# The last tile's mean taken from the matrix product, through two more weight columns

## The reference

```
logits = einsum('bsh,he->bse', hidden_states, gate_w)
routing_weights, _ = top_k(logits, 2)
h = relu(einsum('bsh,hi->bsi', hidden_states, up_w)) ** 2
shared_out = einsum('bsi,ih->bsh', h, down_w)
x_latent = einsum('bsh,hl->bsl', hidden_states, fc1_w)
expert_out = einsum('bsl,lm->bsm', x_latent, expert_w)
moe_out = expert_out * sum(routing_weights, axis=-1, keepdims=True)
routed_out = einsum('bsl,lh->bsh', moe_out, fc2_w)
return _layernorm(shared_out + routed_out, ln_gamma, ln_beta)   # over 512 values
...
x + _L0_ffn_ref(_L0_cond_ref(x, ...), ...)
```

## Time and profile before

| | us |
|---|---|
| median of three runs | 256.61 |
| span of the profiled execution, first to last instruction | 254.6 |
| median of the runs less that span | 2.0 |
| PE busy | 248.0 |
| DVE busy | 155.8 |
| ACT busy | 81.8 |
| POOL busy | 39.4 |

### The profile page before, as it was taken

How to read it: one execution, slowest core, us unless ns; L and a number is a source line. 1 busy time by engine, 2 the same in 40 slices (tenths; PEclk the granted TensorE clock), 3 DMA queues, 4 the chain that set the end, 5 groups by cost and what they waited for, 6 DMA issues and landing times.

```text
span 254.6 us, 3526 instructions
## 1 busy us (share of the span) xinstructions
PE 248.0 (97%) x1291; PEld 207.1 (81%) x1291; DVE 155.8 (61%) x272; ACT 81.8 (32%) x142; POOL 39.4 (15%) x45
## 2 busy tenths in 40 slices
PE   8999999999999999999999999999999999999992
PEld 7877887988888888888888888888888888788891
DVE  4798999944448964644447983464444953406453
ACT  4669856411003452321112534331111355202100
POOL 2400021000117120001114411001111700001110
PEclk9999999999999999999999999999999999999997
DMA  6994804001111400001111220000011100000111
GB/s 161 332 324 153 305 17 153 0 0 44 41 41 41 167 0 0 3 0 42 41 41 41 78 87 0 0 0 11 31 41 44 42 0 0 0 3 8 74 44 41
DMA packets 10444, 15.60 MB, mean 61 GB/s; under 512 B 1088, under 2 KB 4928, under 8 KB 10432
## 3 DMA queue, kind: packets, MB, share of 16 engines
q1 hardware_dynamic: 9984, 15.33, 17.6%
q10 hardware_dynamic: 448, 0.11, 0.2%
HBM read 11.23 MB, written 4.20 MB: 61 GB/s over the span
## 4 chain that ended last, share of the span: by engine, by line
PE 89%; DMA 3%; issue 2%; DVE 1%; SPq 1%; ACT 0%; POOL 0%; POOLq 0%; DVEq 0%
PE ps L932 27%; PE ps L934 27%; PE ps L933 27%; PE ps L906 4%; DMA late<-in_up_w_dram 3%; PE ps L998 2%; PE ps L950 1%; PE ps L956 1%; PE ps L952 1%; SPq L322 0%; POOL rstd L417 0%; DVE stats L714 0%; DVE y_buf L712 0%; DVE h_full L636 0%; ACT h_hi L474 0%
## 5 line engine op out<-in xcount | busy, mean ns | idle before, releaser
L932 PE MATMUL ps<-down_hi,sq_hi 128*128 128x512 f32 (+1 forms) x136 | 51.2, 377 | 0.0
L933 PE MATMUL ps<-down_lo,sq_hi 128*128 128x512 f32 (+1 forms) x136 | 51.2, 377 | 0.0
L934 PE MATMUL ps<-down_hi,sq_lo 128*128 128x512 f32 (+1 forms) x136 | 51.2, 376 | 0.0
L932 PE MATMUL ps<-h_hi,up_hi 128*128 128x512 f32 x120 | 46.8, 390 | 0.0
L934 PE MATMUL ps<-h_hi,up_lo 128*128 128x512 f32 x120 | 46.7, 389 | 0.0
L933 PE MATMUL ps<-h_lo,up_hi 128*128 128x512 f32 x120 | 46.7, 389 | 0.0
L417 POOL TENSOR_TENSOR rstd<-mv,half 128x1 f32<-128x1 f32 x16 | 15.3, 954 | 158.2 <-DVE mv L719 153.2
L512 ACT ACTIVATE relu_sq<-ps 128x512 f32<-128x512 f32 x32 | 19.1, 597 | 57.7 <-PE ps L934 44.3
L712 DVE TENSOR_TENSOR y_buf<-ps,y_buf 128x512 f32<-128x512 f32 x15 | 10.4, 692 | 41.0 <-PE ps L934 40.7
L685 DVE CAST sq_hi<-relu_sq 128x512 fp32r<-128x512 f32 x32 | 22.6, 706 | 16.2 <-ACT relu_sq L514 15.7
L932 PEld LDWEIGHTS ps<-down_hi,sq_hi 128*128 128x128 f32 x136 | 25.6, 188 | 4.7
(11 more groups left out here) (137 smaller groups left out, 308.7 us busy)
## 6 DMA issues: line engine op xcount, KB each, us to landing
out_dram<-late SPq DMA_DIRECT2D x15, 256.0 KB, 2.0
x_cur<-in_x_dram SPq DMA_DIRECT2D x3, 1024.0 KB, 5.2
late<-in_down_w_dram SPq DMA_DIRECT2D x4, 512.0 KB, 5.3
late<-in_up_w_dram SPq DMA_DIRECT2D x3, 512.0 KB, 8.8
x_cur<-in_x_dram SPq DMA_DIRECT2D x2, 512.0 KB, 7.2
experts_sb<-in_experts_dram SPq DMA_DIRECT2D x3, 256.0 KB, 3.5
agg_b<-aggb_dram SPq DMA_DIRECT2D x1, 768.0 KB, 4.9
latents_sb<-in_latents_dram SPq DMA_DIRECT2D x1, 528.0 KB, 4.8
```

What stands on the lines that cost most here:

```text
L932: nc.tensor.matmul(dst, a_hi, b_hi, start=first, stop=False)
L933: nc.tensor.matmul(dst, a_hi, b_lo, start=False, stop=False)
L934: return nc.tensor.matmul(dst, a_lo, b_hi, start=False, stop=last)
```

## The change

The mean of a token over its 512 outputs is the product of its activations with the row sums of the weights, over 512. The change keeps each row sum, split into high and low part and written twice, as columns 512 and 513 of `down_hi`, `down_lo`, `q_hi` and `q_lo`. These rows become 514 values long (2056 bytes in place of 2048). The sums are made by DVE in block 0, between its four `normalise` calls.

In the last tile the half with columns 256 to 511 now comes first, and its 30 products are 258 wide: the two columns more hold the sum over all 512 outputs. The gamma step of this half then needs nothing of the other half. The gamma step of the other half stands right behind the joint statistics and does not wait for them; only `rstd` still does. The order of the two stores is exchanged too.

```diff
+            def sum_rows(weights, at, n, part):
+                nc.vector.tensor_reduce(row_sums[:, part, at:at + n], weights[:, :, 0:HID].bitcast(fp32), AX.X,
+                                        ALU.add).then_inc([hi_summed, lo_summed][part], 1)
+
+            def split_sums():
...
+                nc.vector.tensor_copy(down_hi[:, :, HID:HID + 2], row_sums[:, 0, 0:IC].unsqueeze(2).to_broadcast([P, IC, 2])
+                                      ).then_inc(sum_hi_ready, 1)
...
+                def times_gamma(i):
+                    cols = halves[i]
+                    nc.vector.scalar_tensor_tensor(out=y[:, cols], in0=last_shared(i), scalar=last_mean[:, :],
+                                                   in1=gamma_b[:, cols], op0=ALU.subtract,
+                                                   op1=ALU.mult).then_inc(gamma_done, 1)
...
+                        nc.vector.tensor_scalar(last_mean[:, :], LAST_MEAN, 1.0 / HID, None,
+                                                ALU.mult).then_inc(last_mean_ready, 1)
+                        dve.wait_ge(last_mean_ready, 1)
+                        times_gamma(0)
                 dve.wait_ge(eps_added, 1)
                 dve.wait_ge(stats_done, n + 1)
                 nc.vector.bn_aggr(out=mv[:, :], in_=last_stats[:, :, :]).then_inc(mv_done, 2)
-                dve.wait_ge(mv_done, 2 * n)
-                for i, cols in enumerate(halves):
-                    nc.vector.scalar_tensor_tensor(out=y[:, cols], in0=last_shared(i), scalar=mv[:, 0:1],
-                                                   in1=gamma_b[:, cols], op0=ALU.subtract,
-                                                   op1=ALU.mult).then_inc(gamma_done, 1)
+                times_gamma(1)
...
-            for t in range(TB):
-                normalise(0, t)
+            normalise(0, 0)
+            sum_rows(down_hi, 0, IC, 0)
+            normalise(0, 1)
+            sum_rows(down_lo, 0, IC, 1)
+            normalise(0, 2)
+            sum_rows(q_hi, IC, LC, 0)
+            sum_rows(q_lo, IC, LC, 1)
+            split_sums()
+            normalise(0, 3)
...
                     if last_block and t == TB - 1:
                         pe.wait_ge(last_lo_ready, LC)
+                        pe.wait_ge(sums_ready, 3)
                         for half in (0, 1):
-                            cols = slice(half * HID // 2, (half + 1) * HID // 2)
+                            cols = LAST_COLS[half]
+                            dst = [shared(TB - 1)[:, 0:HID // 2 + 2], last_shared(1)][half]
```

More of the change, by code:

```diff
@@ L88, in adaln_ffn_kernel @@
         up_lo = sb("up_lo", [P, HC, INT], f32r)
-        down_hi = sb("down_hi", [P, IC, HID], f32r)
-        down_lo = sb("down_lo", [P, IC, HID], f32r)
+        down_hi = sb("down_hi", [P, IC, HID + 2], f32r)
+        down_lo = sb("down_lo", [P, IC, HID + 2], f32r)
         fc1_hi = sb("fc1_hi", [P, HC, LAT], f32r)
         fc1_lo = sb("fc1_lo", [P, HC, LAT], f32r)
-        q_hi = sb("q_hi", [P, LC, HID], f32r)
-        q_lo = sb("q_lo", [P, LC, HID], f32r)
+        q_hi = sb("q_hi", [P, LC, HID + 2], f32r)
+        q_lo = sb("q_lo", [P, LC, HID + 2], f32r)
         h_hi = sb("h_hi", [P, HC, TOK], f32r)
@@ L117, in adaln_ffn_kernel @@
         mv = sb("mv", [P, 2])
+        row_sums = sb("row_sums", [P, 2, IC + LC])
+        last_mean = sb("last_mean", [P, 1])
         rstd = sb("rstd", [P, 1])
@@ L202, in routed @@
             return ps[:, 6 + t % 2, :]
+        LAST_COLS = [slice(HID // 2, HID + 2), slice(0, HID // 2)]
         def last_shared(half):
             return [shared(TB - 1), ps[:, LAT_BANK[0], :]][half][:, 0:HID // 2]
+        LAST_MEAN = shared(TB - 1)[:, HID // 2:HID // 2 + 1]
         mlp_loaded = [sem(f"mlp_loaded{i}") for i in range(2)]
@@ L305, in adaln_ffn_kernel @@
         gamma_done = sem("gamma_done")
+        hi_summed = sem("hi_summed")
+        lo_summed = sem("lo_summed")
+        rows_summed = sem("rows_summed")
+        sum_hi_ready = sem("sum_hi_ready")
+        sums_ready = sem("sums_ready")
+        last_mean_ready = sem("last_mean_ready")
         final_done = sem("final_done")
@@ L357, in _ @@
             for half in (0, 1):
-                cols = slice(half * HID // 2, (half + 1) * HID // 2)
+                cols = [slice(HID // 2, HID), slice(0, HID // 2)][half]
                 sp.wait_ge(final_done, NT + half)
@@ L533, in down_high @@
                 act.wait_ge(down_loaded[i], 16)
-                nc.scalar.copy(down_hi[:, ks, :], down_raw[:, ks, :]).then_inc(down_hi_ready, 1)
+                nc.scalar.copy(down_hi[:, ks, 0:HID], down_raw[:, ks, :]).then_inc(down_hi_ready, 1)
             for m in range(IC):
@@ L729, in normalise @@
                                                op1=ALU.add).then_inc(final_done, 1)
+            def sum_rows(weights, at, n, part):
+                nc.vector.tensor_reduce(row_sums[:, part, at:at + n], weights[:, :, 0:HID].bitcast(fp32), AX.X,
+                                        ALU.add).then_inc([hi_summed, lo_summed][part], 1)
+            def split_sums():
+                dve.wait_ge(hi_summed, 2)
+                dve.wait_ge(lo_summed, 2)
+                nc.vector.tensor_tensor(row_sums[:, 0, :], row_sums[:, 0, :], row_sums[:, 1, :], ALU.add
+                                        ).then_inc(rows_summed, 1)
+                dve.wait_ge(rows_summed, 1)
+                nc.vector.tensor_copy(down_hi[:, :, HID:HID + 2], row_sums[:, 0, 0:IC].unsqueeze(2).to_broadcast([P, IC, 2])
+                                      ).then_inc(sum_hi_ready, 1)
+                nc.vector.tensor_copy(q_hi[:, :, HID:HID + 2], row_sums[:, 0, IC:IC + LC].unsqueeze(2).to_broadcast([P, LC, 2])
+                                      ).then_inc(sum_hi_ready, 1)
+                dve.wait_ge(sum_hi_ready, 2)
+                nc.vector.tensor_tensor(down_lo[:, :, HID:HID + 2], row_sums[:, 0, 0:IC].unsqueeze(2).to_broadcast([P, IC, 2]),
+                                        down_hi[:, :, HID:HID + 2].bitcast(fp32), ALU.subtract).then_inc(sums_ready, 1)
+                nc.vector.tensor_tensor(q_lo[:, :, HID:HID + 2], row_sums[:, 0, IC:IC + LC].unsqueeze(2).to_broadcast([P, LC, 2]),
+                                        q_hi[:, :, HID:HID + 2].bitcast(fp32), ALU.subtract).then_inc(sums_ready, 2)
             def normalise_last():
@@ L735, in normalise_last @@
                 y = y_buf[:, t % 2, :]
-                halves = [slice(0, HID // 2), slice(HID // 2, HID)]
+                halves = [slice(HID // 2, HID), slice(0, HID // 2)]
+                def times_gamma(i):
[3 more added lines that the diff above has]
+                                                   op1=ALU.mult).then_inc(gamma_done, 1)
                 for i, cols in enumerate(halves):
@@ L763, in down_low @@
                 dve.wait_ge(down_hi_ready, i + 1)
-                nc.vector.tensor_tensor(down_lo[:, ks, :], down_raw[:, ks, :], down_hi[:, ks, :].bitcast(fp32),
+                nc.vector.tensor_tensor(down_lo[:, ks, 0:HID], down_raw[:, ks, :], down_hi[:, ks, 0:HID].bitcast(fp32),
                                         ALU.subtract).then_inc(down_lo_ready, 1)
@@ L1012, in down_product @@
                         pe.wait_ge(last_lo_ready, LC)
+                        pe.wait_ge(sums_ready, 3)
                         for half in (0, 1):
-                            cols = slice(half * HID // 2, (half + 1) * HID // 2)
+                            cols = LAST_COLS[half]
+                            dst = [shared(TB - 1)[:, 0:HID // 2 + 2], last_shared(1)][half]
                             for lc in range(LC):
-                                three_products(last_shared(half), lat_hi[:, lc, rows], lat_lo[:, lc, rows],
+                                three_products(dst, lat_hi[:, lc, rows], lat_lo[:, lc, rows],
                                                q_hi[:, lc, cols], q_lo[:, lc, cols], lc == 0, False)
                             for m in range(IC):
-                                last = three_products(last_shared(half), sq_hi[:, m, rows], sq_lo[:, m, rows],
+                                last = three_products(dst, sq_hi[:, m, rows], sq_lo[:, m, rows],
                                                       down_hi[:, m, cols], down_lo[:, m, cols],
@@ L1036, in down_product @@
                         last = three_products(shared(t), sq_hi[:, m, rows], sq_lo[:, m, rows],
-                                              down_hi[:, m, :], down_lo[:, m, :], m == 0, m == IC - 1)
+                                              down_hi[:, m, 0:HID], down_lo[:, m, 0:HID], m == 0, m == IC - 1)
                     last.then_inc(shared_done, 1)
```

6 lines of the change are left out of this document (3 added, 3 removed).

## The result

The changed kernel takes 261.04 us (median of 5 runs, 260.62 to 261.26) against 256.63 for the kernel before in the same session (256.14 to 256.71). The ratio is 1.0175, 95% interval 1.0162 to 1.0187. The forecast was 256.4 us, in a range from 255.9 to 257.2: wrong, and on the side of the rival "the shifted rows", which had 0.09. The granted clock of PE is 0.997 in the profiled execution, before 0.995, so the clock does not explain the loss.

The account below looks back on a forecast made before the run. PE, busy 248.0 of 254.6 us, was taken to bound the kernel, leaving its start, products and tail. The tail's -0.22 and wider products' +0.025 gave -0.20, from 256.61 to 256.4 us; range 255.9 to 257.2.

Parts of the forecast that it names:

- the shifted rows: Rival, chance 0.09: products starting off a 16 byte multiple take longer; at the upper bound +3.3 - 0.20, 259.7 us.
- The tail: Behind PE's last product: final steps start 0.22 us earlier, 1.54 us after it, released by POOL's power at 0.55.
- Wider products: Last tile on PE: two columns more in 30 products cost 0.025 us, bounds nothing and 3.2 us.
- DVE in block 0: Sums of 4.38 us delay tile 3's start to near 77.6; PE's slack covers it, price nothing.
- Longer rows: PE's products with q and down read rows 2056 bytes apart, 255 of them odd rows; taken as costing nothing.
- The bound: Upper limit for Longer rows: the fixed part of a product once more, 255 x 0.0128 = 3.3 us.
- The sign of being wrong: Forecast wrong if down stage products stand further apart than up stage ones, PE waits in block 1, or last power takes 0.98.
- The line rule: SBUF lines of 16 bytes: an odd row touches one line more, estimated 0.11 us, making the sum -0.09.
- a part of 0.04: Chance left for what the prediction did not see, with all buffers behind `down_hi` moving by up to 192 bytes.

Follow-up runs that it names:

- e9_rows256: Changed kernel with `down` and `q` rows of 576 values, eight start-up buffers moved into `early`, all operand distances 0 modulo 256 bytes; 256.35 us, ratio 0.9988.
- e1_h_place: Kernel before with one unused buffer of 64 bytes a partition ahead of `h_hi`, moving it and all behind it; 260.49 us, ratio 1.0148.
- e3_rows64: Changed kernel with `down` and `q` rows of 528 values in place of 514, so every row starts on a multiple of 64 bytes; 258.72 us, ratio 1.0087.
- e5_gap128: Kernel before with an unused gap of 128 bytes ahead of `h_hi`, so up, latent and down products are at distance 128; 261.50 us, ratio 1.0205.
- e4_all_place: Kernel before with a 64 byte buffer ahead of the first buffer, so all move together and keep their distances; 256.49 us, ratio 0.9998.
- e2_h_back: Changed kernel with a 64 byte buffer ahead of `h_hi`, putting it and all behind it back on a multiple of 128; 259.20 us, ratio 1.0099.
- e6_gap192: Kernel before with an unused gap of 192 bytes ahead of `h_hi`: up and latent products at distance 192, down at 64; 260.01 us, ratio 1.0137.

## Why the prediction was wrong

- **The tail** was right: 1.53 us against 1.54, the power the last to come, at 0.55, and one gamma step hidden behind PE's second half.
- **Wider products** were right in size: 258 columns cost nothing visible. In `e9_rows256`, where every distance is 0, the half with 258 columns takes 3.59 us, as the one with 256 did before.
- **DVE in block 0** was right: the sum 4.41 us against 4.38; tile 3 at 78.53 against 77.6, and 0.9 of that is PE's lag, with which tile 0 came already (its final step at 58.68 in place of 57.78); no wait of PE.
- **Longer rows** is the step that failed. It put this term of the sum at nothing, where PE's products took some 4.5 us more. It took nothing on the ground that all products shown keep the same distance in time whatever they read. That ground was empty: in the kernel before every pair of operands lies at a distance of 0 modulo 256, so its trace had one case only, and could not tell that the case matters. The step also counted the wrong products. It looked at the odd rows (255) and at the start against a multiple of 16 bytes; the runs show that rows on multiples of 64 lose as much, that one common shift loses nothing, and that all 930 products of 512 columns were at stake, more than half of them (480 up and latent ones) reading nothing that was changed.
- **The bound** of 3.3 us rested on that count, and on an assumed price, the fixed 12.8 ns of a product once more. No mean price in the table is that high; it is the count that took the loss past the bound. With the measured prices it is 384 x 6.5 ns (up) + 96 x 2.1 (latent) + 360 x 4.6 (down) + 90 x 3.9 (q) = 4.7 us. From the chain and the products behind it there are 0.76 + 3.71 + 0.34 = 4.81, or 4.5 without the 0.28 of start-up.
- **The rival of shifted rows**, with 0.09, had the direction and not the mechanism. It has a product slow when its operand starts off a multiple of 16 bytes, but in `e1_h_place`, `e3_rows64` and `e5_gap128` every operand starts on a multiple of 64 bytes, and they lose 2.2 to 5.0 us.
- **The sign of being wrong** would have missed it: it asked whether the down stage stands further apart than the up stage. In the changed kernel it is the other way round, 231.2 against 233.3 ns.
- **The line rule** of the Trainium skill (Advanced Engine Details and Errata, "SBUF Cachelines") gave the direction, but the estimate of 0.11 us made from it is far too small and its form does not fit: 16 byte lines would make no difference between `e1_h_place` and `e4_all_place`, of which one loses 3.9 us and the other nothing.
- The 192 bytes by which all later buffers move were seen, and given a part of 0.04. By `e2_h_back` that was the cause of about 1.8 us of the loss, net.

## What to carry to other kernels

Resizing a buffer moves all that are placed behind it, and that alone can cost more than the edit is worth: 64 unused bytes cost 1.5% here. Where 512 wide products bound the kernel, keep the moving and the stationary operand of each product, and the rows of both, at the same place modulo 256 bytes, or leave a gap behind a resized buffer that restores it. And a trace in which all cases are alike gives no bound for a case that it does not have: test a new layout on its own before the change that needs it.

## What the runs showed of the hardware

- Where all products of a stage have the same distance between the starts of their operands modulo 256 bytes, the time of a 512 wide `fp32r` product depends on it: 226.7 ns at 0, 228.8 to 230.2 at 64, 232.7 at 128, 233.2 to 234.3 at 8, 32, 96, 160, 192 and 224. In a stage with mixed distances the neighbours count too: in `e3_rows64` products at 0 take 230 to 232 ns. The mechanism is not known from these runs.
- Products of 256 or 258 columns showed no such price, and at two distances they were even shorter: the last tile's first half takes 3.57 us in the changed kernel, 3.41 in `e1_h_place` (distance 192), 3.40 in `e6_gap192` (64), against 3.59 before.
- The mixing products (128 columns, plain fp32) take 3.77 us for 32 in the chain of the kernel before and of the changed one alike, though `mix` and `x_cur` moved against each other.
